# Five weight loads on ScalarE's queue and a new order of the opening work: a cross-attention and quantised-FFN kernel

## What is computed

```python
x = x + xattn(layernorm(x), context, Wq, Wkv, Wout, bout)   # queries do not matter: the mask fixes the weights
h = layernorm(layernorm(x)) * gamma + beta
h = gelu(qlinear(h, w1, b1))      # xq = round(h * 127/max|h|), wq = clip(round(w / mean|w|), -1, 1)
x = x + qlinear(h, w2, b2)        # y = xq @ wq / (scales) + b
```

## Time and profile before

| | |
|---|---|
| median of three runs | 539.83 us |
| the profiled execution: its time / its span | 540.51 us / 538.7 us |
| TensorE busy | 527.3 us, 98% of the span |
| VectorE, ScalarE, GpSimd busy | 453.6, 435.9, 407.3 us (84, 81, 76%) |
| DMA | 78.72 MB, mean 146 GB/s; 270 to 410 GB/s in the first 40 us |

### The profile page before, as it was taken

The page is one execution under the profiler, slowest core; times in us unless marked ns, Lnnn a source line. Parts: engine busy times, 40 slices in busy tenths (PEclk is TensorE's granted clock), DMA queues, the critical chain, the costliest instruction groups (busy, mean ns, idle before and its releaser), DMA issues.

```text
span 538.7 us, 8129 instructions
## 1 busy us (share of the span) xinstructions
PE 527.3 (98%) x2434; PEld 227.4 (42%) x2434; DVE 453.6 (84%) x758; ACT 435.9 (81%) x444; POOL 407.3 (76%) x533
## 2 busy tenths in 40 slices
PE   9979989999999999999999999999999999999997
PEld 5433434444444444444444444444444444444443
DVE  3877999999989899988888887988888889887653
ACT  3558899888887888888888888888888889887762
POOL 2288687999998888888888988888888888873300
PEclk9987999999999999999999999999999999999999
DMA  8999233886565656555665556665455574535433
GB/s 310 402 387 294 69 69 102 170 208 162 135 122 141 131 148 119 129 125 130 131 143 142 123 129 117 141 132 132 124 123 130 129 142 103 92 86 100 95 78 98
DMA packets 137015, 78.72 MB, mean 146 GB/s; under 512 B 114246, under 2 KB 114310, under 8 KB 136972
## 3 DMA queue, kind: packets, MB, share of 16 engines
q1 hardware_dynamic: 135636, 75.80, 57.3%
q10 hardware_dynamic: 1335, 2.41, 1.3%
HBM read 33.88 MB, written 17.05 MB: 95 GB/s over the span
## 4 chain that ended last, share of the span: by engine, by line
PE 95%; DVE 3%; POOL 1%; ACT 1%; issue 1%; POOLq 0%; DVEq 0%; ACTq 0%
PE py L1055 41%; PE p L1040 28%; PE pab L1040 14%; PE p L983 3%; PE p L1030 3%; PE pab L1008 2%; PE pab L1030 1%; POOL xr L387 1%; PE pab L968 1%; DVE hx L792 1%; PE py L1016 1%; PE py L1008 1%; DVE w2q L779 1%; ACT hid L578 0%; PE py L974 0%
## 5 line engine op out<-in xcount | busy, mean ns | idle before, releaser
L1055 PE MATMUL py<-w2q,hqT 128*128 128x512 bf16 x1024 | 231.0, 379 | 1.7 <-DVE hqT L829 1.7
L587 ACT ACTIVATE hq<-hid,hscale 128x2048 int8<-128x2048 f32 x64 | 128.1, 2002 | 46.2 <-DVE hscale L821 46.2
L1040 PE MATMUL p<-w1q,xqT 128*128 128x512 bf16 x688 | 159.4, 380 | 0.0
L1055 PEld LDWEIGHTS py<-w2q,hqT 128*128 128x128 bf16 x1024 | 100.1, 98 | 123.0 <-DVE hqT L829 2.7
L578 ACT ACTIVATE hid<-p,xdeq 128x1024 f32<-128x1024 f32 x86 | 95.0, 1106 | 15.9 <-PE p L1040 11.2
L1040 PEld LDWEIGHTS p<-w1q,xqT 128*128 128x128 bf16 x688 | 63.8, 98 | 81.2 <-issue 10.1
L387 POOL TENSOR_TENSOR xr<-xr,attn 128x512 f32<-128x512 f32 x64 | 83.3, 1320 | 18.7 <-DVE attn L727 17.2
L402 POOL TENSOR_TENSOR hx<-hx,beta_b 128x512 f32<-128x512 f32 x64 | 91.7, 1454 | 4.4 <-ACT hx L563 4.3
L815 DVE TENSOR_REDUCE hmax<-hid 128x1 f32<-128x1025 f32 x64 | 78.1, 1220 | 18.0 <-ACT hid L578 17.4
L406 POOL TENSOR_TENSOR xr<-xr,b_b 128x512 f32<-128x512 f32 x64 | 92.6, 1465 | 0.0
L809 DVE TENSOR_REDUCE hid<-hid 128x1 f32<-128x1024 f32 x64 | 77.4, 1209 | 8.8 <-ACT hid L578 8.8
(11 more groups left out here) (88 smaller groups left out, 408.9 us busy)
## 6 DMA issues: line engine op xcount, KB each, us to landing
xr<-x SPq DMA_DIRECT2D x64, 256.0 KB, 2.9
out<-xr SPq DMA_DIRECT2D x64, 256.0 KB, 2.4
raw<-w1T SPq DMA_DIRECT2D x8, 512.0 KB, 12.2
hid<-wvT SPq DMA_DIRECT2D x8, 256.0 KB, 7.8
wout<-wout_d ACTq DMA_DIRECT2D x8, 256.0 KB, 8.7
wout<-w2T SPq DMA_DIRECT2D x3, 512.0 KB, 5.5
xr<-w2T SPq DMA_DIRECT2D x2, 512.0 KB, 11.1
attn<-ctxm_d SPq DMA_DIRECT2D x4, 256.0 KB, 8.1
```

The source lines that it names most:

```text
L587: nc.scalar.activation(hq8[:, t % 2, :], hid[:, t % 2, 0:HID], ACT.Copy, scale=col(hscale, t))\
L1040: mm = nc.tensor.matmul(hidden_bank(t, n), xT[:, k, :], w1q[:, k, n * D:(n + 1) * D], start=False, stop=(k == KD - 1))
L1055: mm = nc.tensor.matmul(py[:, t % 2, :], hqT[:, t % 2, c // 2, c % 2, :], w2q[:, c, :], start=(c == 0), stop=(c == 2 * NJ - 1))
```

## The change

SP no longer issues pieces 0 to 4 of w2. ScalarE issues them on its own DMA queue, two behind `abs_w1(5)`, two behind `abs_w1(6)`, one behind `abs_w1(7)`. In SP's list w1's last two pieces go ahead of x tile 3, and the context right behind that. VectorE's list puts `weight_sum(0)`, `weight_scale(0)` and the rounding and clipping of w1 ahead of the work for later tiles; ScalarE's puts `round_x(0)`, `round_x(1)` and its two quarters of w1 there, with `copy_wvo(3)` between the two, and spreads the sums of |w2| around the gelus of tile 0. On TensorE only `out_rows(0)` and `out_rows(1)` stay ahead of the first layer of tile 0, `out_rows(2)` follows it, `tail_product` and `out_rows(3)` change places, and `out_rows` waits for `wvo` piece by piece. GpSimd's list is re-ordered to match. The arithmetic is the same.

```diff
--- before.py
+++ after.py
@@ -207,8 +207,6 @@
                     .then_inc(w1_loaded[i], 16)
 
             def load_w2(j):
-                if j == 3:
-                    sp.wait_ge(mean_done, 1)
                 if j == 5:
                     sp.wait_ge(wvo_done, KD)
                 sp.dma_start(w2raw[j], w2T[j * 2 * P:(j + 1) * 2 * P, :].rearrange("(p e) n -> p e n", e=2))\
@@ -286,40 +284,35 @@
             load_w1(4)
             load_w1(5)
             sp.dma_start(beta_b[:, :], beta.partition_broadcast(P)).then_inc(beta_loaded, 16)
-            load_x(3)
             load_w1(6)
             load_w1(7)
+            load_x(3)
+            load_ctx()
+            load_b1_rows()
             load_x(4)
-            load_w2(0)
-            load_b1_rows()
             load_x(5)
-            load_w2(1)
-            load_ctx()
-            load_w2(2)
             load_x(6)
-            load_w2(3)
-            load_w2(4)
             transpose_x(0)
             load_w2(5)
             load_w2(6)
+            transpose_x(1)
             load_w2(7)
             load_x(7)
             load_x(8)
             load_x(9)
+            transpose_x(2)
+            transpose_x(3)
             sp.dma_start(b2_b[:, 0, :], b2.partition_broadcast(P)).then_inc(b2_loaded, 16)
             load_x(10)
-            transpose_x(1)
             load_x(11)
             load_x(12)
             load_x(13)
-            transpose_x(2)
-            transpose_x(3)
+            transpose_h(0)
+            load_x(14)
+            load_x(15)
+            transpose_h(1)
             transpose_x(4)
-            transpose_h(0)
             transpose_x(5)
-            load_x(14)
-            transpose_h(1)
-            load_x(15)
             transpose_h(2)
             sp.wait_ge(tail_copied, 1)
             sp.dma_start(tail_rows, tail_out).then_inc(tail_stored, 16)
@@ -440,37 +433,37 @@
             pool.wait_ge(mean_copied, 1)
             add_attention(0, 1)
             add_attention(1, 1)
-            add_attention(2, 1)
-            add_attention(3, 1)
             pool.wait_ge(const_set, 3)
             inverse_std(0, 1)
+            add_attention(2, 1)
             inverse_std(1, 1)
             pool.wait_ge(beta_loaded, 16)
             add_beta(0, 1)
-            inverse_std(2, 2)
-            add_attention(4, 1)
             add_beta(1, 1)
-            add_attention(5, 1)
+            add_attention(3, 1)
             widen_x(0, 1)
             pool.wait_ge(wscale_done[0], 1)
             scale_rows(0, 1)
+            inverse_std(2, 2)
+            widen_x(1, 1)
+            scale_rows(1, 1)
             add_beta(2, 1)
             add_beta(3, 1)
+            add_attention(4, 1)
+            scale_rows(2, 2)
+            add_attention(5, 1)
+            add_attention(6, 1)
+            widen_x(2, 2)
             inverse_std(4, 2)
-            scale_rows(1, 1)
-            add_attention(6, 1)
-            widen_x(1, 1)
+            add_attention(7, 1)
             add_beta(4, 1)
             add_beta(5, 1)
-            scale_rows(2, 2)
-            widen_x(2, 2)
-            add_attention(7, 1)
             add_attention(8, 1)
             scale_rows(4, 2)
             add_attention(9, 1)
+            inverse_std(6, 2)
             pool.wait_ge(b2_loaded, 16)
             add_b2(0)
-            inverse_std(6, 2)
             add_attention(10, 1)
             add_attention(11, 1)
             widen_x(4, 2)
@@ -526,6 +519,13 @@
             for m in range(KI):
                 act.dma_start(wout[:, m, :], wout_d[m * P:(m + 1) * P, :]).then_inc(chunk_loaded[m], 16)
 
+            def load_w2(j):
+                if j == 3:
+                    act.wait_ge(mean_done, 1)
+                act.dma_start(w2raw[j], w2T[j * 2 * P:(j + 1) * 2 * P, :].rearrange("(p e) n -> p e n", e=2))\
+                    .then_inc(w2_loaded[j], 16)
+
+
             def first_gelu():
                 act.wait_ge(const_set, 2)
                 nc.scalar.activation(wpart[:, 0, 6:8], neg_half[:, :], ACT.Gelu).then_inc(vmean_done, 1)
@@ -613,52 +613,57 @@
             abs_w1(3)
             times_std(0)
             abs_w1(5)
-            copy_wvo(2)
+            load_w2(0)
+            load_w2(1)
             times_std(1)
             abs_w1(6)
+            load_w2(2)
+            load_w2(3)
+            copy_wvo(2)
             abs_w1(7)
+            load_w2(4)
             round_x(0)
+            round_x(1)
+            round_weights(0, 1)
+            copy_wvo(3)
+            round_weights(0, 3)
             times_std(2)
             times_std(3)
             abs_w2(0)
-            copy_wvo(3)
-            round_weights(0, 1)
-            round_weights(0, 3)
             abs_w2(1)
-            times_std(4)
-            times_std(5)
-            round_x(1)
             abs_w2(2)
+            abs_w2(3)
+            gelu(0, 0)
             abs_w2(4)
-            abs_w2(3)
+            gelu(0, 1)
+            round_x(2)
+            round_x(3)
             abs_w2(5)
             abs_w2(6)
             abs_w2(7)
-            gelu(0, 0)
-            round_x(2)
-            gelu(0, 1)
-            round_x(3)
-            round_weights(1, 0)
-            round_weights(1, 1)
-            round_x(4)
-            round_x(5)
             gelu(1, 0)
             gelu(1, 1)
+            round_weights(1, 0)
+            times_std(4)
+            times_std(5)
+            round_weights(1, 1)
             round_h(0)
             round_weights(1, 2)
             round_weights(1, 3)
+            gelu(2, 0)
             round_weights(1, 4)
-            gelu(2, 0)
-            times_std(6)
             gelu(2, 1)
             round_h(1)
             round_weights(1, 5)
+            round_x(4)
+            round_x(5)
+            widen_h(0)
             round_weights(1, 6)
-            widen_h(0)
             round_weights(1, 7)
-            times_std(7)
             gelu(3, 0)
             gelu(3, 1)
+            times_std(6)
+            times_std(7)
             round_h(2)
             widen_h(1)
             gelu(4, 0)
@@ -865,61 +870,61 @@
             dve.wait_ge(gamma_loaded, 16)
             centre(0)
             statistics(1)
+            centre(1)
+            abs_w1(4)
             statistics(2)
-            statistics(3)
-            abs_w1(4)
-            centre(1)
             centre(2)
             x_scale(0, 1)
+            weight_sum(0)
+            x_scale(1, 1)
+            weight_scale(0)
+            round_w1(0)
+            clip(0, 0)
+            statistics(3)
             centre(3)
-            statistics(4)
-            weight_sum(0)
-            centre(4)
-            weight_scale(0)
-            statistics(5)
-            x_scale(1, 1)
+            clip(0, 1)
+            round_w1(2)
+            clip(0, 2)
+            clip(0, 3)
+            attn_rows(0)
             ctx_sum(0)
             ctx_sum(1)
             ctx_sum(2)
+            x_scale(2, 2)
+            ctx_sum(3)
+            attn_rows(1)
+            half_scale(0)
+            ctx_means()
+            hidden_scale(0)
+            statistics(4)
+            weight_sum(1)
+            centre(4)
+            weight_scale(1)
+            attn_rows(2)
+            statistics(5)
             centre(5)
-            x_scale(2, 2)
-            attn_rows(0)
-            ctx_sum(3)
-            round_w1(0)
-            round_w1(2)
-            clip(0, 0)
-            clip(0, 1)
-            clip(0, 2)
-            clip(0, 3)
-            attn_rows(1)
-            attn_rows(2)
-            weight_sum(1)
-            ctx_means()
-            weight_scale(1)
-            x_scale(4, 2)
-            half_scale(0)
+            half_scale(1)
+            hidden_scale(1)
+            clip(1, 0)
+            clip(1, 1)
             statistics(6)
             statistics(7)
-            hidden_scale(0)
-            half_scale(1)
+            x_scale(4, 2)
+            tail_rows_out()
+            clip(1, 2)
+            clip(1, 3)
+            half_scale(2)
+            hidden_scale(2)
+            clip(1, 4)
+            clip(1, 5)
+            widen_h(0)
+            attn_rows(3)
+            clip(1, 6)
+            clip(1, 7)
+            centre(6)
             statistics(8)
             statistics(9)
-            hidden_scale(1)
-            centre(6)
             centre(7)
-            half_scale(2)
-            attn_rows(3)
-            tail_rows_out()
-            hidden_scale(2)
-            clip(1, 0)
-            clip(1, 1)
-            clip(1, 2)
-            clip(1, 3)
-            widen_h(0)
-            clip(1, 4)
-            clip(1, 5)
-            clip(1, 6)
-            clip(1, 7)
             statistics(10)
             centre(8)
             statistics(11)
@@ -998,13 +1003,13 @@
 
             def out_rows(i):
                 b = (i + 1) % B
-                pe.wait_ge(wvo_copied, KD)
                 if i == 2:
                     pe.wait_ge(attn_copied, 1)
                 if i == 3:
```

(9 more changed lines are left out.)

## The result

| | before | after |
|---|---|---|
| median of 13 runs each | 539.84 us (538.29 to 542.01) | 546.20 us (541.86 to 547.48) |
| the profiled execution: time / span | 540.51 / 538.7 us | 544.60 / 542.8 us |

The ratio is 1.0102, 95% interval 1.0075 to 1.0129. The forecast was 543.2 (538.5 to 545.0): slower, as forecast, but 6.4 us slower and not 3.4, and the median is above the range.

The account below looks back on a forecast made before the run. TensorE, busy 98% of the span, bounds; time moves by what statistics(10) moves by. First gelu 53.2 + 28.4 = 81.6, + 3.8 = 85.4, 3.4 us later than 82.0: median 539.83 becomes 543.2 us, range 538.5 to 545.0.

Parts of the forecast that it names:

- Up to the products' end: Opening: weight_sum(0) near 34.2 us, first product pause gone, TensorE's products ended at 36.5; a gain.
- The context rows: Loads for out_rows(0): w2 on ScalarE's queue is served first, so the context lands at 41.8 us, before 39.0; a loss.
- The clock: TensorE's pause from 36.5 to 41.8 us: the clock falls again, out_rows(0) and (1) take 9.30 us.
- PEclk 0.50 in it: Sign of being right: granted clock at its lower level in TensorE's 5 us pause and for some us behind.
- G: Start of the first gelu, gelu(0, 0), on ScalarE; forecast at 53.2 us.
- Rival (a): The clock stays up: out_rows(0) and (1) take 7.3 us, first gelu two earlier, 541.2 us; chance 0.1.
- First gelu: gelu(0, 0) at 53.2 us: rows at 41.8, plus 9.3 and 0.3, first layer at 51.4, 1.74 for its first half.
- From G on ScalarE sets the pace: ScalarE's list up to round_weights(1, 7): 26.9 us plus a 1.45 wait, ending 28.4 behind the first gelu, at 81.6.
- The failed step: VectorE behind w2's last rounding: clip, two centrings, two statistics take 3.8 us, so statistics(10) at 85.4.
- (c): Faster: ScalarE's queue doesn't hold up SP's loads; first gelu 48.5, time 538.5 us; decides below 49.8; chance 0.15.
- (b): Queues share bytes evenly, clock up: context rows at 40.2, first gelu 49.6, time 539.6 us, no change; chance 0.08.
- (d): Another wait at 36 us hides all of it, VectorE's list from 82.01 met as before; 539.8 us; chance 0.07.

Follow-up runs that it names:

- the two openings with w2 issued late: The change with VectorE's tiles ahead and GpSimd's betas earlier (543.37 us), and the change with GpSimd's attention additions earlier; w2 first issued at 29.41 and 31.03 us.
- w2 behind the context: The change with w2's first five loads back in SP's list, right behind the context and bias loads; 1.0021 to before, median 540.95 us.
- before with the clock kept: The kernel before with seven products of ones in TensorE's pause ahead of weight_total(0); 0.9982 to before, median down by 1.2 us.
- before with the second queue: The kernel before with only w2's first five loads moved from SP's list to ScalarE's queue; 0.9991 to before.

## Why the prediction was right, and where it was wrong

*Up to the products' end: right.* `weight_sum(0)` came at 33.88 (forecast 34.2), the products ended at 36.8 (36.5), and the product pause was gone. One cost was too high: ScalarE's DMA issues were priced at 0.66 us each. They took 0.33 to 0.46, beside its own operation, and the two that stand behind `abs_w1(5)` in the list went out before that sum began at 28.14. Two rows of its timeline:

```profile
27.52 0.72 ACT L563 ACTIVATE hx<-hx,rstd 128x512 f32<-128x512 f32 x1 [2.23 <-POOL rstd L387]
27.52 0.34 ACTq L525 DMA_DIRECT2D xr<-w2T  x1
```

*The context rows: right as to what, 1.8 us off in the first profile.* Forecast 41.8; 40.00, 41.53, 42.18 and 41.80 in four executions. That w2 is served first holds. A fixed landing time was the wrong picture: it hangs on when SP comes to its last context issue and on how soon behind it ScalarE comes to w2.

*The clock: right in its price.* The same price, 9.3, was taken; 8.83, 9.63, 9.09 and 9.61 were measured. The sign "PEclk 0.50 in it" failed in the first profile, where the whole pause of 3.23 us was at the full clock. And some runs have no such pause: in the two openings with w2 issued late the batches took 7.13 and 7.03 us. By time = G + 493.5 their G of 48.33 and 49.80 give 541.8 and 543.3. The change's lower group of runs lies at 541.7 to 542.4, where the first of these falls; the second falls between the groups. That this group is such an opening is argued: no profile of the unmodified change fell into it. Rival (a), 541.2, is thus near to what a third of the runs do.

*First gelu: right in three profiles of four.* 53.2 forecast; 51.08, then 53.41, 53.53 and 53.67.

*From G on ScalarE sets the pace: right, and 0.5 short.* w2's last rounding ends at 79.95, G + 28.9 (28.4).

***The failed step* is the next one: "Behind it VectorE still has one clip (1.43/4), two centrings and two statistics before `statistics(10)`: 0.4 + 2 x 0.82 + 2 x 0.9 = 3.8".** It measured 6.2 (79.95 to 86.14): 0.4 until the clip before was done, 1.2 for the clip, 3.0 for the centrings, 1.6 for the statistics. The durations came from rows of another stretch, without a look at what GpSimd did there and here. Here it had two attention additions, a cast and three b2 additions beside them. The prediction said "The centrings may be longer" and gave 544.6 for that, but as an upper end; and it priced the clip at a quarter of the row at 80.67. The trace of before had four clips of the same shape at nearly twice that, just ahead of them, with a beta addition on GpSimd beside them (77.75 us):

```profile
77.40 2.75 DVE L779 TENSOR_SCALAR w2q<-w2q 128x1024 bf16<-128x1024 int16 x4
```

With 3.0 and 1.2 in place of 1.64 and 0.4 the forecast would have been 545.4, and the measured median 0.8 from it. (The 544.6 for long centrings is 544.8 by its own numbers: 543.2 + 2 x 0.78.)

*The books.* Forecast for the profiled execution 543.9 = 53.2 + 490.7; the change is G + 493.5. That is 2.8 missing, of which 2.4 are this term (6.2 for 3.8) and the rest ScalarE's list. In the first profile G was 2.1 early, by luck of its opening, which hid most of it (544.6). For the median run, which has no profile, 546.2 less 493.5 would be a G of 52.7. So 3.0 us are missed in the median: 2.8 behind G, less 0.5 for G, plus the 0.7 that was taken off because before's profiled execution lay above its median.

*The rivals.* (c) is what w2 behind the context does: the context at 37.0 and G at 47.41, 1.1 better than (c) had it, and still 540.95 and not below before. Its deciding point, G below 49.8, was wrong by the same term: 540.5 less 493.5 is 47.0. (b) had the bytes wrong, and its 40.2 is given without a working; (d) found no other wait. The range was too narrow above since the long clips were never in it.

*Where the gain went.* The change starts the first layer 6.5 us earlier (G 51.08, not 57.61) and still loses. Before, time less G is 482.9; in the change 493.5. The tile work that filled VectorE while it waited for G now follows w2's clips, 10.6 us more behind G. No variant turned the opening's gain into a shorter time: with G from 45.8 to 57.8 none is clearly faster than before, and the lowest, before with the clock kept (0.9982) and before with the second queue (0.9991), leave the order of the other work as it was. That VectorE and GpSimd can't follow is shown where a wait was traced (the betas); that no order of the lists could do better is not.

## What to carry to other kernels

Before giving loads to a second queue, look at what else is in flight and needed next: the queue with the larger packets takes the bytes, and whoever waits for the small ones pays. When an edit moves work on one engine, price each operation by the rows in which the same neighbour is at work on the other engine, and not by the mean; here the neighbour was a factor of about two for the centrings and three for the clips. And when times fall into two groups, find the event that time less that event is constant for, and compare variants by it.

## What the runs showed of the hardware

- A clip of 128x1024 took 0.41 to 0.43 us alone and 1.2 to 1.5 beside a GpSimd addition or cast; a centring 0.73 to 0.75 alone and up to 1.75. The Trainium skill ("SBUF — State Buffer", section "SBUF: two separate sides") has one port pair that the two use in turn, a whole instruction at a time; the clips agree with it, as they end at 80.46 and 81.64, each 0.28 us behind GpSimd's addition and cast (80.18, 81.36).
- An opening whose w1 sum was 1.9 us late ended 2.7 us earlier, since the same lateness held back the second queue's loads (first issue at 29.41 and not 27.52); with the loads alone issued at 29.93 and 33.93 the rows started at 37.02 and not 40.0 to 42.2.
- The packets of two DMA queues came in equal number, 69 and 69 in a us, though they held 0.28 MB on the one and 0.12 MB on the other. A 256 KB piece of the context took 13.75 us to land beside w2's packets and 8.6 before.
- The five loads issued by ScalarE took 0.33 to 0.46 us each and ran beside its activation, the first two ahead of a sum that stands before them in its list (issued at 27.52 and 27.89, the sum at 28.14).
